# Idle-time transposes ahead of the first image, and the last image's final convolution cut into 128-pixel tiles

## The reference

```
x = x + mix(groupnorm(x))         # relu(cosine similarity of all pixel pairs)^2 times a 1x1 convolution (W, b)
x = x + deform(groupnorm(x))      # offset = conv3x3(conv3x3(h, w1, b1), w2, b2): 72 channels
                                  # val[k] = bilinear sample of h at pixel + tap k + offset, 9 taps, 4 groups
                                  # out = relu(sum over k of wd[k].T @ val[k])
```

## Time and profile before

| | us |
|---|---|
| median of 3 runs | 480.82 (479.06 to 482.84) |
| the profiled execution | 482.29 |
| its span, first to last instruction | 480.57 |
| TensorE busy | 419.0 (87% of the span) |
| VectorE busy | 343.5 (71%) |
| ScalarE busy | 230.3 (48%) |
| GpSimd busy | 131.6 (27%) |
| mean granted clock of TensorE | 0.966 of full speed |

### The profile page before, as it was taken

One profiled execution on the slowest core, in us unless ns is written; L12 is line 12 of the kernel. 1 busy time (PEld: TensorE's weight loads), 2 busy tenths in 40 slices (PEclk: granted clock), 3 DMA queues, 4 the chain that ended last, 5 costly groups with the idle time before them and its releaser, 6 DMA issues.

```text
span 480.6 us, 9714 instructions
## 1 busy us (share of the span) xinstructions
PE 419.0 (87%) x3881; PEld 297.0 (62%) x3881; DVE 343.5 (71%) x582; ACT 230.3 (48%) x412; POOL 131.6 (27%) x171
## 2 busy tenths in 40 slices
PE   2987999989996987999999689798778979888996
PEld 2654657646663755778666466577556657756665
DVE  5993776849999996298754988197987819599401
ACT  3442245155555464242665554434754453278650
POOL 4562471004882112012764110201220120032100
PEclk9997999999999899799999999999999997999999
DMA  7100000021111111211111111402211140032211
GB/s 267 45 1 0 0 1 1 0 50 23 23 23 24 22 23 29 45 24 45 22 23 23 24 24 23 95 12 55 46 23 23 24 88 21 33 63 51 45 35 35
DMA packets 22186, 17.23 MB, mean 36 GB/s; under 512 B 1980, under 2 KB 20668, under 8 KB 22140
## 3 DMA queue, kind: packets, MB, share of 16 engines
q1 hardware_dynamic: 22076, 16.46, 14.7%
q10 hardware_dynamic: 64, 0.13, 0.2%
HBM read 3.74 MB, written 3.28 MB: 15 GB/s over the span
## 4 chain that ended last, share of the span: by engine, by line
PE 51%; DVE 29%; ACT 7%; issue 5%; SPq 3%; DMA 2%; ACTq 1%; POOL 1%; DVEq 0%
PE psB L752 13%; PE psB L524 9%; DVE wpix L1398 6%; PE psV L726 6%; PE psT L703 5%; PE psA L524 5%; PE psA L615 4%; ACT wcell L945 3%; DVE combo L1187 3%; DVE tent L1379 2%; PE psT L693 2%; ACT val L958 2%; SPq L312 2%; DVE tent L1373 2%; DVE combo_p L1191 2%
## 5 line engine op out<-in xcount | busy, mean ns | idle before, releaser
L945 ACT ACTIVATE wcell<-psT 128x512 f32<-128x512 f32 (+1 forms) x160 | 83.3, 552 | 74.3 <-PE psT L703 72.2
L1398 DVE TENSOR_TENSOR wpix<-tent 128x512 f32<-128x512 f32 (+1 forms) x160 | 103.6, 700 | 13.7 <-PE psT L703 12.6
L703 PE MATMUL psT<-ident,wpix 128*128 128x128 f32 x576 | 87.3, 283 | 15.1 <-ACT wcell L945 13.9
L703 PEld LDWEIGHTS psT<-ident,wpix 128*128 128x128 f32 x576 | 66.8, 145 | 39.5 <-issue 31.8
L466 POOL COPY strips<-hring 128x256 f32<-128x256 f32 x64 | 41.5, 676 | 143.6 <-PE psT L693 143.6
L443 POOL TENSOR_TENSOR sim<-rel 128x512 f32<-128x512 f32 x48 | 61.6, 1303 | 68.2 <-ACT rel L895 68.2
L752 PE MATMUL psB<-val,wd_sb 128*128 128x256 f32 x288 | 70.1, 399 | 0.0
L752 PEld LDWEIGHTS psB<-val,wd_sb 128*128 128x128 f32 x288 | 55.6, 198 | 11.8 <-issue 4.0
L958 ACT ACTIVATE val<-psV 128x576 f32<-128x576 f32 x64 | 43.9, 687 | 23.7 <-PE psV L726 21.3
L615 PE MATMUL psA<-sim,scratch 128*128 128x512 f32 x96 | 47.5, 619 | 0.7 <-POOL sim L443 0.6
L726 PE MATMUL psV<-wcell,hwin 64*32 64x144 f32 x2048 | 47.6, 296 | 0.0
(11 more groups left out here) (187 smaller groups left out, 489.8 us busy)
## 6 DMA issues: line engine op xcount, KB each, us to landing
hwin<-hwin SPq DMA_DIRECT2D x64, 128.0 KB, 2.5
out<-yout SPq DMA_DIRECT2D x16, 128.0 KB, 1.8
x_all<-x SPq DMA_DIRECT2D x1, 1536.0 KB, 10.0
off_scr<-sim SPq DMA_DIRECT2D x4, 288.0 KB
combo<-sim SPq DMA_DIRECT2D x32, 32.0 KB
val<-w SPq DMA_DIRECT2D x1, 576.0 KB, 5.9
wd_sb<-wd SPq DMA_DIRECT2D x1, 576.0 KB
x_all<-x SPq DMA_DIRECT2D x1, 512.0 KB, 3.5
```

What stands on the lines that cost most here:

```text
L703: last = pe.transpose(bank[:, at:at + P], wpix[:, t % 2, k, 2 * h:2 * h + 2, :].rearrange("p g q -> p (g q)"), ident[:, :])
L945: act.activation(wcell[:, t % 2, taps[0]:taps[-1] + 1, :, :].rearrange("q k h p -> q (k h p)"), bank[:, 0:len(taps) * G // 2 * P], ACT.Cop ...
L1398: dve.tensor_tensor(w, ty, tx, ALU.mult).then_inc(s["weights_done"], 1)
```

## The change

At the start, `keep_busy` issues transposes of the identity into psV, which nothing reads: 12 before the first `first_mean`, 3 between the two means and 15 after the second.

For the last image, `dconv` is replaced by `dconv_tile`: one 128-pixel tile at a time, in the order 1, 2, ..., 7, 0, and each in two pieces (taps 0 to 4 and 5 to 8; for tile 0 taps 4 to 8 and then 0 to 3). The first pieces of tiles 1 to 5 stand at k = 5 of t = 3..7, the second pieces of tiles 1 to 4 at k = 1 of t = 4..7. The other pieces stand behind the last slot. Relu, addition and store go by the same tiles; four of the relus stand at k = 4 of t = 4..7.

```
+        LAST_ORDER = (1, 2, 3, 4, 5, 6, 7, 0)
+        LAST_TAPS = [(range(5), range(5, K))] * (ROWT - 1) + [(range(4, K), range(4))]
+        LAST_AT = {K * (i + 3 + h) + (1 if h else 5): (i, h) for i in range(5) for h in range(2) if i + h < 5}
...
+            def dconv_tile(i, taps):
+                j = LAST_ORDER[i]
+                bank = (psB, psA)[i // 2 % 2][:, i % 2, 0:P]
+                if taps[0] == LAST_TAPS[i][0][0]:
+                    if i < 2:
+                        pe.wait_ge(s["orelu_done"], 4 * LAST + ORELU0)
+                    elif i == 2:
+                        pe.wait_ge(s["far_all_done"], 1)
+                    elif i >= 4:
+                        pe.wait_ge(s["orelu_done"], 4 * LAST + i - 3 + ORELU0)
+                if j == 0 and taps[0] == 0:
+                    pe.wait_ge(s["val_wrapped"], 2 * LAST + 2)
+                else:
+                    tile = min(j if taps[-1] <= K // 2 else j + 1, ROWT - 1)
+                    pe.wait_ge(s["val_free"], VGROUPS * (ROWT * LAST + tile + 1) + VAL0)
+                if j == ROWT - 1 and taps[-1] == K - 1:
+                    pe.wait_ge(s["val_wrapped"], 2 * LAST + 1)
+                for k in taps:
+                    at = TURN + P * j + shift(k)
+                    last = pe.matmul(bank, wd_sb[:, k * C:(k + 1) * C], val[:, k, at:at + P],
+                                     start=k == LAST_TAPS[i][0][0], stop=k == LAST_TAPS[i][-1][-1])
+                if taps == LAST_TAPS[i][-1]:
+                    last.then_inc(s["dconv_done"], 1)
...
+                        if b == LAST:
+                            if n in LAST_AT:
+                                i, h = LAST_AT[n]
+                                dconv_tile(i, LAST_TAPS[i][h])
...
+                if b == LAST:
+                    sample(b, ROWT - 1, 0)
+                    dconv_tile(4, LAST_TAPS[4][1])
+                    sample(b, ROWT - 1, 1)
+                    for i in (5, 7):
+                        dconv_tile(i, LAST_TAPS[i][0])
+                    for i, h in ((5, 1), (6, 0), (6, 1), (7, 1)):
+                        dconv_tile(i, LAST_TAPS[i][h])
+                    return
...
+            def keep_busy(count):
+                for i in range(count):
+                    pe.transpose(psV[:, 0, 0:P], ident[:, :], ident[:, :])
...
+            keep_busy(12)
             for step in range(2):
                 first_mean(0, 1, step)
+                keep_busy((3, 15)[step])
...
+            def relu_tile(i):
+                act.wait_ge(s["dconv_done"], 4 * LAST + i + 1 + DCONV0)
+                act.wait_ge(s["yout_done"], 4 * LAST + i - 1 + YOUT0)
...
+            def add_tile(i):
+                j = LAST_ORDER[i]
+                dve.wait_ge(s["orelu_done"], 4 * LAST + i + 1 + ORELU0)
+                dve.wait_ge(out_sems[i % 2], 16 * (2 * LAST + i // 2 + 1))
```

More of the change, by code:

```diff
@@ L289, in mix_deform_kernel @@
         DCONV0_AT = (60, 61)
+        LAST = B - 1
+        LAST_ORDER = (1, 2, 3, 4, 5, 6, 7, 0)
+        LAST_TAPS = [(range(5), range(5, K))] * (ROWT - 1) + [(range(4, K), range(4))]
+        LAST_AT = {K * (i + 3 + h) + (1 if h else 5): (i, h) for i in range(5) for h in range(2) if i + h < 5}
+        OUTS = 2 * LAST + QT // 2 + 1
         TURNED0, SAMPLED0, FREE0, VAL0, YOUT0, DCONV0, ORELU0 = 1, 3, 2, 1, 2, 1, 2
@@ L362, in cross, with store_tile @@
                         .then_inc(s["crossed_odd" if t % 2 else "crossed_even"], 16)
+            def store_tile(i):
+                j = LAST_ORDER[i]
+                sp.wait_ge(s["yout_done"], 4 * LAST + i + 1 + YOUT0)
+                sp.dma_start(out[LAST:B, :, BLK * j:BLK * (j + 1), :].rearrange("b c h w -> c (b h w)"),
+                             yout[:, i % 2, 0:P]).then_inc(out_sems[i % 2], 16)
             def store(b, m):
@@ L375, in _ @@
                     shift_offsets(b + 1)
+                else:
+                    store_tile(0)
                 cross(b, ROWT - 1)
-                for m in range(4):
-                    store(b, m)
+                if b == LAST:
+                    for i in range(1, QT):
+                        store_tile(i)
+                else:
+                    for m in range(4):
+                        store(b, m)
             for half in range(2):
-                sp.wait_ge(out_sems[half], 16 * (2 * B + 1))
+                sp.wait_ge(out_sems[half], 16 * OUTS)
             sp.wait_ge(s["off_saved"], 16 * B)
@@ L809, in batch_steps @@
                             sample(b, t - 1, SAMPLE_SLOT[k])
-                        if n in DCONV0_AT:
+                        if b == LAST:
+                            if n in LAST_AT:
+                                i, h = LAST_AT[n]
+                                dconv_tile(i, LAST_TAPS[i][h])
+                        elif n in DCONV0_AT:
                             first = 3 * DCONV0_AT.index(n)
@@ L964, in relu_out @@
                     .then_inc(s["orelu_done"], 1)
+            def relu_tile(i):
+                act.wait_ge(s["dconv_done"], 4 * LAST + i + 1 + DCONV0)
+                act.wait_ge(s["yout_done"], 4 * LAST + i - 1 + YOUT0)
+                act.activation(orelu[i % 2][:, 0:BLK, :],
+                               (psB, psA)[i // 2 % 2][:, i % 2, 0:P].rearrange("p (r c) -> p r c", c=WID), ACT.Relu)\
+                    .then_inc(s["orelu_done"], 1)
             def general_path():
@@ L1003, in batch_steps @@
                             conv_front(nxt, n, STEADY)
+                        if b == LAST and t >= 4 and k == 4:
+                            relu_tile(t - 4)
+                if b == LAST:
+                    take_samples(b, ROWT - 1, 0)
+                    relu_tile(4)
+                    take_samples(b, ROWT - 1, 1)
+                    for i in range(5, QT):
+                        relu_tile(i)
+                    return
                 relu_out(b, 0)
@@ L1408, in add_out @@
                     .then_inc(s["yout_done"], 1)
+            def add_tile(i):
+                j = LAST_ORDER[i]
+                dve.wait_ge(s["orelu_done"], 4 * LAST + i + 1 + ORELU0)
+                dve.wait_ge(out_sems[i % 2], 16 * (2 * LAST + i // 2 + 1))
+                dve.tensor_tensor(yout[:, i % 2, 0:P].rearrange("p (r c) -> p r c", c=WID), orelu[i % 2][:, 0:BLK, :],
+                                  batch(x_all, LAST)[:, j * P:(j + 1) * P].rearrange("p (r c) -> p r c", c=WID), ALU.add)\
+                    .then_inc(s["yout_done"], 1)
             def find_farthest():
@@ L1452, in general_path @@
             def general_path():
-                dve.wait_ge(out_sems[0], 16 * (2 * B + 1))
+                dve.wait_ge(out_sems[0], 16 * OUTS)
                 dve.wait_ge(s["stat2_done"], 2 * B)
@@ L1510, in batch_steps @@
                                 weights(nxt, 0, i)
+                if nxt is None:
+                    for i in range(QT):
+                        add_tile(i)
+                    return
                 add_out(b, 0)
```

## The result

| | before | after |
|---|---|---|
| median of 6 runs | 480.91 us (479.04 to 482.84) | 475.72 us (474.13 to 477.46) |
| ratio | | 0.9868 (95%: 0.9828 to 0.9909) |
| span of the profiled execution | 480.6 us | 475.2 us |

The change makes the kernel faster: the medians are 5.2 us (1.1%) apart, and the ratio, 0.9868, would be 6.3 us (4.4 to 8.3 by its interval). The forecast was 474.3 with a range of 472.2 to 477.8.

What follows compares the result with a forecast made beforehand. In the last image no engine was full, TensorE and ScalarE alternating; at the start VectorE led, then TensorE from 38.58 us. Last image -5.3 and start -1.2 make -6.5 from 480.82: 474.3 us, range 472.2 to 477.8.

Steps and rivals of the forecast that it cites:

- Rival E: Last image: loads bound a 128-column pass; above 0.15 us a record the gain is gone, at 0.19 486 us; chance 4%.
- D: Last image: pieces not hidden, each pushes ScalarE's chain back by its full length; 479 to 481 us; chance 8%.
- Step 2 of the working: Last image, loop: TensorE's own time for a tile is 3.76 of 5.19 us, leaving 1.43 us of room.
- Step 4: Last image, behind loop: psV wait 0.86 us, -5.1 us. Start: earlier squares delay diagonal 0.8 to 1.8 us, clock falls.
- Step 5: Last image: smaller relu and addition, -0.2 us. Start: slow stretch behind 38.58 us may go, -3.1 to +2, taken -1.2 us.
- Step 1: Start: the 12 transposes run at 1.2 GHz to about 6.3 us, delaying the first mean by 0.25 us.
- Step 2: Start: clock at 2.4 GHz between 7 and 10 us, product in 1.9 us; 0.27 us wait goes, 0.25 delay comes: nothing.
- Step 3: Start: transposes can raise TensorE's clock; after 27 transposes at 0.50 it was at 1.00 right behind.
- Rival B: The start changes nothing, as clock and gap stay or a new dip is absorbed; 475.5 us (474.9 to 476.5); chance 25%.

Runs made afterwards that it cites:

- `long_turns`: The changed kernel with 60 transposes of the identity in place of 15 ahead of the first product; 482.2 us, timed once.
- `fill_gap`: The changed kernel plus 32 transposes of the identity in TensorE's idle gap ahead of the second `first_mean`; ratio 0.9878 to the kernel before.
- `late_gap`: The changed kernel plus 32 transposes ahead of the second `first_mean`, and tile 5's first piece moved into the wait for psV; ratio 0.9887 to the kernel before.
- `conv_only`: The changed kernel without the transposes at the start, only the tiled convolution of the last image; ratio 0.9909 to the kernel before, again 0.9920.

## Why the prediction was right, and where it was off

*The range and the sign held.* 475.72 lies in 472.2 to 477.8, and the gain was 5.2 us by the medians, 6.3 by the ratio, for a forecast of 6.5. Both terms had the right sign: the last image -4.3 us in the profile (forecast -5.3, range -2.7 to -6), the start -1.9 and -3.1 us alone in two measurements (forecast -1.2, range -3.1 to +2). These don't sum to 5.2 exactly, and the intervals of each are over 1 us wide. That the sum came so near is in part luck: the last image gave 1.0 us less than forecast, and the start, whose chain of steps failed, gave more.

*Both signs of being wrong came.* The prediction called itself wrong if the tile period was over 6.1 us, and it is 6.12, or if the clock still fell at 38 us behind a gap of 4 us, and it did: at 36.7 us, in a gap of 4.23 us. The first is an error of size, 0.27 us a tile; the second is the failure of the mechanism at the start.

*The last image: right mechanism, three terms off.* TensorE is full in every tile, as forecast, and its own sum sets the period.
- The price of a record, 0.112 us, held: four taps in 444.18 to 445.18, five in 447.29 to 448.40. Rival E (loads bound a 128-column pass) is refuted, and so is D: nothing was hidden only in half.
- Step 2 of the working: the period was to be 5.85 and is 6.12. The mis-sized term is the 0.07 us for changes between kinds of matmul. From the starts: eight transposes 0.93 (counted 0.90), four taps 1.00 (0.90), four transposes 0.53 (0.45), eight again 0.93, five taps 1.11 (1.12), two transposes 0.32 (0.22). In all 0.34 where 0.07 stood (two sample halves at 0.65 as counted); over four tiles 1.1 us.
- Step 4: the wait cost 1.0 (forecast 0.86), and the last 27 matmuls 6.3 in place of 6.05, since the last record's own run through the engine was not counted. Together 0.4.
- Step 5: from the end of TensorE's work to the end of the span it was 4.59 us and is 3.89: -0.7 where I took -0.2. Relu and addition were 0.28 and 0.29 as taken; the smaller last store was worth the 0.5 that I had set to nothing (from the last addition to the end of the span 3.7 to 4.6 us in the four profiles with stores of 256 pixels, 3.1 to 3.6 in the ten with 128). The store of the sixth tile was not waited for.

These errors sum to +1.5 - 0.5 = +1.0 us, which is the difference of 5.3 and 4.3 (61.27 us from the start of image 3 to the end in the profile before, 56.93 after).

*The start: the sign and the range held, the mechanism did not.*
- Step 1 held in its bounds: the first mean starts at 6.11, 0.06 later than before.
- Step 2 failed. The clock should have been up at 7 to 10 us and VectorE's wait gone. In eight of ten profiles it rose at 11.2 to 12.9, 7.7 to 9.3 us after TensorE's first transpose, where I had carried over the 3.4 and 6.1 us of two other places; in the two others it rose after 2.9 and 3.4 us. The 15 transposes then stand in the way of the product (10.99 instead of 9.68).
- Step 3 held: the clock rises behind transposes (`long_turns`, 6.4 us) and stays up through them (`fill_gap`). The page "TensorE: Matmul & The Clock Gate" of the Trainium skill, section on the PE-mode transpose, says that the full clock doesn't engage for them; for f32 transposes these two runs contradict it, with 60 transposes at 0.112 us each and four products at 1.96 us behind 32 transposes.
- Step 4, squares start early and push the diagonal back, so that TensorE's clock falls in a gap of over 3 us: in the changed kernel nothing of it happened (squares at 17.02, a gap of 1.42 us). In `late_gap`, with an early clock, the squares did start at 15.46, yet the diagonal ended at 19.7 as ever. The clock did fall there, at 13.7 and 20.5, but not by my chain: the first time TensorE had had no idle time behind 7.4 us.
- Step 5, the fall behind 38 us may be spared: it was not in the changed kernel. In profiles with added transposes or products it lasted 3.4 us six times and 6.8 us twice where the gap was left open, against 6.8 in all four without. That would be 3.4 / 2 x 6 / 8 = 1.3 us, but in three of the six a dip near 100 us, which no profile without transposes has, took as much again. Why the dip is shorter is not shown.
- What the runs show instead: without transposes the clock stayed low to 22 us in two of four profiles, which delays VectorE's run by 2 us; with them it never did. If that is a matter of the execution, half of 2 us is 1 us on average. Measured were 1.9 and 3.1. The rest may lie in the shorter dip behind 38 us, or behind 113 us in later dips, whose lengths differ between executions of one kernel. How much each gives stays open, and so does whether the kernel before ever rises late.

Rival B (the start changes nothing) was the reading of the profile alone, and gave 475.5, nearest to the measured median. The two halves measured apart speak against it.

## What to carry to other kernels

Where two engines alternate and each waits for the other, add up what the fuller one does in a period: the room for filler is the period less that sum, and it lies at each wait, so filler has to be cut and put at each of them. Price each change between kinds of matmul: here the eight in a tile cost from nothing to 0.10 us each, 0.34 in all. One profile shows one moment of the clock: before an effect at the start of a kernel is priced, read the start of several executions.

## What the runs showed of the hardware

- The clock can fall, and stay low, with TensorE busy: in `late_gap` it rose at 6.9 and fell at 13.7, with TensorE busy for all of 9.5 to 13.8 (product, norms and the first scores). In `conv_only` it stayed low from 9.6 to 22.0 through 3.6 us of product, 3.3 us of norms and 5.3 us of scores without a pause.
- With a gap of 4.2 us filled with 3.65 us of transposes the clock stayed at full (`fill_gap`; `late_gap` too). Left open, the gap was followed by half rate in all twelve profiles: in six of them the clock fell within the gap, for 6.8 us, and in six from about its end to 1.1 us behind it, for 3.4 us.
- Of 2.3 us gained by 113 us of a 475 us kernel, 1.6 vanished at 190 us in a dip of the clock that the profile of the changed kernel doesn't have there.
